# Router weights from a GpSimd power during the expert tiles, and a last stage whose first block is mixed ahead of two shared copies

## The reference, cut to what matters

```python
logits = r @ codebook.T / TEMP              # TEMP = 0.7
vals, idx = top_k(softmax(logits), 2)
w = vals / sum(vals)                        # the two router weights
eo = silu(h @ W1[e] + b1[e]) @ W2[e] + b2[e]        # per chosen expert
shared = (silu(h @ Ws1 + bs1) @ Ws2 + bs2) * 0.25
hmoe = w[0] * eo[idx[0]] + w[1] * eo[idx[1]] + shared
f = silu(layernorm(hmoe) @ Wf1 + bf1) @ Wf2 + bf2
out = x + hmoe + f
```

## Time and profile before

| | |
|---|---|
| median of 3 runs | 890.82 us (890.13 to 891.63) |
| the profiled execution | 891.35 us, of which span 889.5 us |
| mean granted clock of PE | 0.956 of full speed |
| PE busy | 788.0 us (89%) |
| DVE busy | 659.6 us (74%) |
| ACT busy | 656.9 us (74%) |
| POOL busy | 324.7 us (36%) |

### The profile page before, as it was taken

One profiled execution on the slowest core, in us unless ns is written; L12 is line 12 of the kernel. 1 busy time (PEld: TensorE's weight loads), 2 busy tenths in 40 slices (PEclk: granted clock), 3 DMA queues, 4 the chain that ended last, 5 costly groups with the idle time before them and its releaser, 6 DMA issues. The chain is left out here.

```text
span 889.5 us, 22649 instructions
## 1 busy us (share of the span) xinstructions
PE 788.0 (89%) x7286; PEld 607.1 (68%) x7286; DVE 659.6 (74%) x2165; ACT 656.9 (74%) x1498; POOL 324.7 (36%) x397
## 2 busy tenths in 40 slices
PE   0857998998989989899899999987889999999798
PEld 0534665765766656667656666664779999999687
DVE  2997899999999999999999999553423344443675
ACT  1775999999898988998999999765335565655444
POOL 3110124334343353343433523444414545555121
PEclk9978999999999999999999999997889999999899
DMA  8129889889899889898898898894089999995411
GB/s 163 49 55 210 189 191 208 193 188 212 188 204 206 183 180 206 181 204 187 182 210 176 187 206 181 196 208 102 21 279 387 376 395 403 324 360 191 149 30 36
DMA packets 82305, 177.77 MB, mean 200 GB/s; under 512 B 8244, under 2 KB 35339, under 8 KB 82240
## 3 DMA queue, kind: packets, MB, share of 16 engines
q1 hardware_dynamic: 65536, 164.01, 73.9%
q0 software_dynamic: 5760, 7.92, 2.7%
q10 hardware_dynamic: 10944, 5.02, 2.1%
HBM read 65.93 MB, written 113.34 MB: 202 GB/s over the span
## 5 line engine op out<-in xcount | busy, mean ns | idle before, releaser
L879 DVE TENSOR_TENSOR arena<-qT,b_qk 128x2304 f32<-128x2304 f32 x128 | 323.8, 2543 | 1.6 <-DVE v_bias L904 0.3
L615 ACT ACTIVATE arena<-arena 128x2304 f32<-128x2304 f32 x128 | 271.6, 2122 | 41.8 <-DVE arena L879 40.9
L1324 PE MATMUL b_s<-arena,apad 128*32 128x192 f32 x3072 | 160.4, 345 | 30.9 <-ACT p L624 24.2
L760 ACT ACTIVATE act_h<-big,arena 128x128 f32<-128x128 f32 x336 | 96.1, 369 | 74.1 <-PE big L1641 69.7
L1324 PEld LDWEIGHTS b_s<-arena,apad 128*32 128x32 f32 x3072 | 90.5, 113 | 87.8 <-issue 43.0
L541 POOL TENSOR_TENSOR kept<-kept,rs 96x384 f32<-96x384 f32 x64 | 52.7, 824 | 215.0 <-DVE rs L1026 214.8
L589 POOL DMA_INDIRECT eo_dram<-gT,toff x84 | 82.5, 983 | 96.3 <-issue 64.3
L658 ACT ACTIVATE kept<-kept,mx 96x96 f32<-96x96 f32 x256 | 92.3, 365 | 11.9 <-DVE mx L1019 11.3
L1641 PE MATMUL big<-hbT,arena 128*128 128x128 f32 x672 | 91.2, 280 | 2.3 <-DVE hbT L1207 1.2
L1641 PEld LDWEIGHTS big<-hbT,arena 128*128 128x128 f32 x672 | 83.6, 196 | 3.1 <-issue 2.1
L1207 DVE TENSOR_SCALAR hbT<-b_t,cols 128x128 f32<-128x128 f32 x84 | 34.4, 409 | 65.0 <-PE b_t L1634 65.0
(11 more groups left out here) (209 smaller groups left out, 1441.4 us busy)
## 6 DMA issues: line engine op xcount, KB each, us to landing
rows_dram<-act_h SPq DMA_DIRECT2D x32, 3096.0 KB
arena<-in_wpack SPq DMA_DIRECT2D x84, 578.0 KB
prT<-rows_dram ACTq DMA_DIRECT2D x76, 64.5 KB
arena<-eo_dram SPq DMA_DIRECT2D x4, 512.0 KB, 6.9
x_dram<-res SPq DMA_DIRECT2D x16, 96.0 KB
out<-of SPq DMA_DIRECT2D x12, 128.0 KB, 1.8
eo_dram<-gT,toff POOLq DMA_INDIRECT x84
rows_dram<-rows_now,slot_now POOLq DMA_INDIRECT x64
```

The costliest lines, as they stand in the source:

```text
L615: act.activation(v, v, ACT.Tanh).then_inc(s["tanh"], 1)
L760: last = act.activation(act_h[:, i, c * TILE:(c + 1) * TILE], big[i][:, c * TILE:(c + 1) * TILE], ACT.Silu, bias=wslot[:, slot, 2 * DFF + ...
L879: dve.tensor_tensor(ring[c % TRING].rearrange("p (x m n) -> p x m n", m=CQ, n=N), qv.unsqueeze(3).to_broadcast([D, SPLIT * QG, CQ, N]), kv ...
L1324: last = pe.matmul(b_s[32 * a:32 * a + 32, 0:SPLIT * N], apad[:, 31 - line:63 - line], t[:, :, a, m, :], start=(line == 0), stop=(line == ...
```

## The change

- POOL fills a new tile `base_e` (128 x 24) with exp(1 / 0.7), once, near its start.
- POOL makes `gap_e` = base_e ** gaps_t (a tensor_tensor with the power operation, 128 x 24) right behind `store_rows(12)`. ACT's exponential and its two table loads are gone.
- DVE makes the weights in three pieces, one each at the end of its turns 15, 16 and 17 of the tiles. The first waits for `gap_e`.
- In the last stage DVE copies shared blocks 8 and 9, starts `mixture(0)`, and copies shared blocks 10 and 11 in the middle of it, between the residual and the wait for POOL's 1/sqrt.
- PE's wait for all shared copies moves from ahead of the first `f_turn(0)` to ahead of the first multiplication by Wf2.

```diff
+            pool.memset(base_e[:, :], float(np.exp(1.0 / TEMP)))
...
+            def weigh():
+                pool.wait_ge(s["gaps_t"], 1)
+                pool.tensor_tensor(gap_e[:, :], base_e[:, :], gaps_t[:, :], ALU.pow).then_inc(s["gap_e"], 1)
+
             for t in range(FIXED):
                 store_rows(t)
+                if t == RELAY + 3:
+                    weigh()
...
-            act.wait_ge(s["gaps_t"], 1)
-            act.preload_act_table(ACT.Exp)
-            act.activation(gap_e[:, :], gaps_t[:, :], ACT.Exp, scale=1.0 / TEMP).then_inc(s["gap_e"], 1)
-            act.preload_act_table(ACT.Silu)
...
+            def weights(i):
+                if i == 0:
+                    dve.wait_ge(s["gap_e"], 1)
+                    ch.link(dve.tensor_scalar(gaps_t[:, :], gap_e[:, :], 1.0, None, ALU.add))
+                elif i == 1:
+                    ch.wait()
+                    ch.link(dve.reciprocal(wts[:, :, 0], gaps_t[:, :]))
+                else:
+                    ch.wait()
+                    ch.link(dve.tensor_tensor(wts[:, :, 1], gap_e[:, :], wts[:, :, 0], ALU.mult))
...
                 if t == RELAY + 2:
                     take_relaid()
+                if RELAY + 6 <= t < RELAY + 9:
+                    weights(t - RELAY - 6)
...
-            for j in range(NB - SHARED_LATE, NB):
+            for j in range(NB - SHARED_LATE, NB - 2):
                 shared_rows(j)
-            dve.wait_ge(s["gap_e"], 1)
-            ch.link(dve.tensor_scalar(gaps_t[:, :], gap_e[:, :], 1.0, None, ALU.add))
-            ch.wait()
-            ch.link(dve.reciprocal(wts[:, :, 0], gaps_t[:, :]))
-            ch.wait()
-            ch.link(dve.tensor_tensor(wts[:, :, 1], gap_e[:, :], wts[:, :, 0], ALU.mult))
-            ch.wait()
...
                 ch.link(dve.tensor_tensor(rh[j % RESIDUALS], hm[:, :, :], xr[:, j, :].rearrange("p (g d) -> p g d", g=G),
                                           ALU.add))
+                if j == 0:
+                    for i in range(NB - 2, NB):
+                        shared_rows(i)
                 dve.wait_ge(s["frstd"], j + 1)
...
             def last2(j):
-                if not (known(j) and j == 0):
+                if known(j) and j == 0:
+                    pe.wait_ge(s["ysh"], NB)
+                else:
                     pe.wait_ge(s["of"], j)
...
-            pe.wait_ge(s["ysh"], NB)
             f_turn(0)
```

More of the change, by code:

```diff
@@ L176, in program @@
         gap_e = sb("gap_e", [128, NT])
+        base_e = sb("base_e", [128, NT])
         wts = sb("wts", [128, NT, TOPK])
```

## The result

The change makes the kernel slower: 892.50 us against 890.13 us (medians of 22 runs each), ratio 1.0031 with a 95% interval of 1.0015 to 1.0046. Of 890 us that is +2.8 us, between +1.3 and +4.1. Forecast were +3.3 us, 894.1 us in a range of 891.1 to 898.2. Single runs of either kernel differ by some 9 us, so the interval of the ratio says more than a median.

What follows compares the result with a forecast made beforehand. PE bounds the tiles, DVE's order the last stage. Stall +4.3, clock +1.4 and last-stage gain -2.4 make +3.3 us on 890.82: 894.1 us, range 891.1 to 898.2.

Steps and rivals of the forecast that it cites:

- The stall: Tiles, tile 16: DVE waits in turn 15 for POOL's power, its hbT comes late, and PE loses 4.3 us.
- the three turns in the code are one turn in time: Tiles: tile 12's store waits for DVE's turn 14 copy; power starts at 688.05, DVE asks at 688.10.
- Cover and semaphores: Tile 16: the part of the power that costs PE nothing, 0.7 us, including 0.1 us of DVE cover.
- P: Length of POOL's 24-column power behind tile 12's store: taken as 5.0 us, with 4.4 and 5.6 as bounds.
- my three ways to go from 96 to 128 partitions: Power's length from earlier rows: partitions cost once 4.4 us, every column dearer 5.0, only columns grow 5.6.
- rival 1: Turn 15: the power hardly grows with columns, about 0.8 us, so no stall; 888.4 us, faster; chance 0.09.
- The clock: Tiles after the stall: PE's clock falls to 0.50 for 2.8 us of work, losing 1.4 us.
- Rival 2: Tile 16: the stall passes without a fall of the clock, +1.9 us, 892.7 us; chance 0.17.
- The wider bound (3.3): Tiles after the stall: the dearer clock case, low for about 6.7 us, costing PE 3.3 us.
- The last stage: Block 0 starts 2.55 us earlier, at 828.45 in place of 831.00; gain 2.4 us, bounds 0.8 and 3.4.
- copy 9, load, copies hidden: Last stage: second shared copy done at 827.37, load landed at 828.41, two moved copies hidden but for 0.1 to 0.2 us.
- PE's clock: Last stage: if PE runs that stretch at low clock, it did so before too; no cost counted.

Runs made afterwards that it cites:

- the power twice: Against the change: POOL makes the 24-column power twice in a row, first into a tile nobody reads; 895.66 us against 888.49 us, ratio 1.0100.
- before, again: The kernel before, unedited, run once more for a second profile; 888.91 us, one run.
- the change, again: The changed kernel, unedited, measured once more beside the kernel before, with a second profile; 890.43 us against 888.49 us, ratio 1.0016.
- only the order: Against the change: no power, exponential and weight operations in their old places, last two shared copies still inside block 0; 887.66 us against 886.85 us, ratio 1.0000.

## Why the prediction was right

**The stall.** The step that the three turns in the code are one turn in time held to a tenth: the power was to start at 688.05 by the earlier trace rows and started at 687.85 in a profile that runs 0.1 us ahead; DVE asked 0.1 us after that. Cover and semaphores were 0.97 us together, not 0.7: P is 4.23, the stall 3.26. P itself I had taken as 5.0 from 4.4 to 5.6. Of my three ways to go from 96 to 128 partitions, the one by which partitions cost only once (4.4) was the nearest, and I had taken another; the extra 0.1 us of the 128x2 row is no matter of columns. The term was forecast at 4.3 and measured at 3.3, the largest error of the sum.

**The rule on elementwise operations** (rival 1, the Trainium skill's GPSIMD Engine Reference, section 3.1) does not hold for powers: 153 to 158 ns for a column of 128 partitions, where the multiplication over 384 columns takes 824 ns in all. The page's figure is for additions, and the rows of powers in the trace before told the two apart.

**The clock.** Forecast 1.4 us lost, as after the idle time at 829.86; measured 1.74, 1.74 and 1.73 in the three profiles with a pause of 3.1 us. (The 0.69 of 839.0 to 839.5 in the earlier trace rows puts the rise at about 839.3, so my price from that row should have been 2.9 us at half speed, 1.45.) The clock fell in all three and did not in the one with 1.2 us. Rival 2 got 0.17; nothing speaks for it at this length. The wider bound (3.3) was nearly reached by the power twice, with 3.0.

**The last stage.** Forecast -2.4 us. Block 0's start came nearer to the last tile by 3.35 us in the first pair of profiles and by 2.6 to 3.4 us over all. The sum's working was right in kind (copy 9, load, copies hidden), but its first number was an accident: the load's issue at 825.61 was 4.09 us behind the last copy, where seven of ten profiles have 3.33 to 3.36. In the kernel before nothing depended on it, since the exponential held block 0 to 831.00; so there was nothing in that trace to show that it was late. Part of the gain goes again: block 2's `fn` comes 4.19 us after block 1's in every kernel with early weights, 3.82 and 3.81 in the kernel before. PE's clock has a share too, which I had taken to be the same on both sides. In three profiles it stood at 0.50 until 10 to 11 us after the start of block 0, and block 3's `fn` came 4.54 us (before, again), 4.41 (the change, again) and 4.42 (only the order) after block 2's in place of 4.20; in the first of them DVE waited 0.24 us for PE's output of block 0. In the other seven it was back by 9 us or hadn't fallen, and nothing was lost. By the end of the span the stage has gained 2.9 us in the first pair, 2.3 in the second.

**The sum.** +3.3 was 4.3 + 1.4 - 2.4; the first profiles say 3.26 + 1.74 - 2.88 = +2.1 us, the spans +2.0, and the runs +2.8 (1.3 to 4.1). The stall was forecast 1.0 us too long and the gain 0.5 too small, and the clock's 0.3 went the other way. So the three terms and the path were right, but by the profiles the sum is 1.2 us too high; that it lies within 0.5 us of the first runs is luck, and the second runs of the same pair say +1.4.

## What to carry to other kernels

A distance in an order written out by hand must be counted in time, from the event that releases the producer to the consumer's place in its own queue: "after tile 12" and "in turn 15" were 0.14 us apart (687.85 and 687.99). A small operation that nothing needs soon can be asked for on a busy engine's queue much later, or made on the other engine earlier, at no cost; asked for a moment too early, it charges nearly its whole length (3.3 of 4.2 us here) to whatever stands behind the question. Where that is TensorE, a fall of the clock can come on top: 1.7 us behind a pause of 3.1, nothing behind one of 1.2. And when a wait is removed, the event that was hidden behind it becomes the bound, so its time in one profile is worth less than it looks.

## What the runs showed of the hardware

- A GpSimd power on 128 partitions takes 0.80 us for 2 columns, 2.33 for 12 and 4.23 for 24 (a second one right behind it 4.15). The first had -0.5 for every exponent, the others a different one for every element; a column costs the same from 2 to 12 as from 12 to 24. ACT makes the same 24 columns of exponentials in 0.22 us, between two table loads of 1.28 us.
- The price of a fallen clock isn't one number. After a pause of 1.2 us there was none, after 3.1 us it was 1.7 us three times, after 7.2 us 3.0 us, since PE then worked at half speed for 6 us before the clock rose.
- In two of ten profiles PE stood still for 1.1 us in the tiles, about 75 us after the first tile's copy before, 81 in the change (5 of them its stall), at the same tile. DVE had written that tile's `hbT` late, 2.19 us after its last work in place of 0.71, and ACT's silu was late too; POOL's stores and the DMAs went on. The second profiles of both kernels don't have it, so it is nothing of the change. I did not find its cause.
- The extra 0.37 us in block 2, in all six kernels with early weights and with the old as with the new order of the copies, also stays open. In the change DVE stands idle for 0.53 us before the aggregate (line 1287), behind its own statistics, where it is 0.15 us at most in the kernel before. It wasn't tried apart.
